# Moving the choice weights, the second score and the row scatter within a step of an attention and expert pipeline

## The reference

```python
x = x + tanh(g_xattn) * cross_attention(layernorm(x), ctx, mask, Wq, Wkv)
x = x + tanh(g_ffn) * experts(layernorm(x), w_router, fc1, fc2, gate_w, up_w, down_w)
```

## Time and profile before

| what | us |
|---|---|
| median of 3 executions | 374.56 |
| lowest and highest | 373.56, 378.98 |
| profiled execution | 375.32 |
| its span in the profile | 373.5 |
| TensorE busy | 312.4 (84%) |
| VectorE busy | 261.0 (70%) |
| ScalarE busy | 170.3 (46%) |
| GpSimd busy | 117.3 (31%) |

### The profile page before, as it was taken

One profiled execution on the slowest core, in us unless ns is written; L12 is line 12 of the kernel. 1 busy time (PEld: TensorE's weight loads), 2 busy tenths in 40 slices (PEclk: granted clock), 3 DMA queues, 4 the chain that ended last, 5 costly groups with the idle time before them and its releaser, 6 DMA issues.

```text
span 373.5 us, 7926 instructions
## 1 busy us (share of the span) xinstructions
PE 312.4 (84%) x2404; PEld 253.7 (68%) x2405; DVE 261.0 (70%) x778; ACT 170.3 (46%) x325; POOL 117.3 (31%) x130
## 2 busy tenths in 40 slices
PE   1827898988998785787979957999898998999994
PEld 1625777776877664553427546888787887888884
DVE  5565587888999698875637996666575665744786
ACT  2413667766675362463355502544343543434231
POOL 4131211216171525234340080564334343332000
PEclk9958999999999896989989996999999999999998
DMA  7728465656569555211020410233233232310783
GB/s 222 207 64 214 113 189 166 182 167 189 175 174 312 164 171 145 94 52 58 34 80 0 119 54 15 85 94 94 85 93 107 72 99 72 96 39 7 237 321 112
DMA packets 34912, 46.44 MB, mean 124 GB/s; under 512 B 5599, under 2 KB 29539, under 8 KB 34370
## 3 DMA queue, kind: packets, MB, share of 16 engines
q1 hardware_dynamic: 28434, 29.17, 27.8%
q10 hardware_dynamic: 2992, 8.32, 6.9%
q0 software_dynamic: 3456, 8.56, 6.7%
HBM read 21.55 MB, written 12.62 MB: 91 GB/s over the span
## 4 chain that ended last, share of the span: by engine, by line
PE 51%; DVE 19%; SPq 11%; DMA 8%; issue 5%; ACT 5%; POOL 1%; DVEq 0%; POOLq 0%; ACTq 0%
PE ps L1462 30%; SPq L345 5%; DMA stacks<-work 4%; SPq L352 4%; PE ps L1350 4%; DVE fc_lo L1049 3%; DVE mx L828 3%; PE ps L1512 3%; DVE fc_lo L1043 2%; PE ps L1428 2%; PE ps L1282 2%; PE ps L1266 2%; PE ps L1184 2%; PE ps L1233 2%; DMA stacks<-mx_t 1%
## 5 line engine op out<-in xcount | busy, mean ns | idle before, releaser
L514 POOL DMA_INDIRECT expert_rows<-v_s,slot_u x39 | 38.3, 982 | 76.8 <-ACT v_s L741 61.1
L828 DVE TENSOR_REDUCE mx<-ps 128x8 f32<-128x1024 f32 x32 | 39.2, 1224 | 16.1 <-PE ps L1233 15.4
L487 POOL TENSOR_TENSOR work<-work 128x512 bf16<-128x512 f32 x16 | 18.5, 1156 | 75.3 <-ACT work L565 75.3
L1462 PE MATMUL ps<-fc_hi,xs_hi 128*128 x78 | 35.3, 452 | 6.2 <-DVE xs_lo L1071 6.2
L1090 DVE TENSOR_TENSOR probs<-ps,probs 128x256 f32<-128x256 f32 x39 | 16.6, 425 | 32.9 <-ACT probs L734 32.8
L596 ACT ACTIVATE probs<-ps 128x1024 f32<-128x1024 f32 x32 | 32.6, 1019 | 13.4 <-PE ps L1266 13.2
L479 POOL DMA_INDIRECT dispatched<-row_s,slot_u x32 | 31.8, 992 | 19.7 <-DVE dest_f L924 10.7
L734 ACT ACTIVATE probs<-ps 128x256 f32<-128x256 f32 x39 | 15.0, 384 | 49.6 <-PE ps L1462 49.6
L1462 PE MATMUL ps<-fc_lo,xs_hi 128*128 x78 | 31.8, 407 | 0.0
L1462 PE MATMUL ps<-fc_hi,xs_lo 128*128 x78 | 31.5, 404 | 0.0
L1233 PE MATMUL ps<-stacks 96*128 96x128 bf16 x256 | 20.6, 225 | 11.3 <-DMA stacks<-work 6.2
(11 more groups left out here) (195 smaller groups left out, 808.4 us busy)
## 6 DMA issues: line engine op xcount, KB each, us to landing
stacks<-work SPq DMA_DIRECT2D x96, 128.0 KB, 3.0
probs<-dispatched SPq DMA_DIRECT2D x39, 129.0 KB, 2.1
fc_s<-in_fc ACTq DMA_DIRECT2D x8, 512.0 KB, 3.5
stacks<-expert_rows SPq DMA_DIRECT2D x4, 1024.0 KB, 6.1
fc_s<-in_fc ACTq DMA_DIRECT2D x8, 256.0 KB, 4.2
ctx_s<-in_ctx_t SPq DMA_DIRECT2D x8, 192.0 KB, 3.2
x_all<-in_x SPq DMA_DIRECT2D x1, 1536.0 KB, 9.1
out<-x_all SPq DMA_DIRECT2D x3, 512.0 KB, 6.7
```

The source lines that it names most:

```text
L487: nc.gpsimd.tensor_tensor(out[:, 2, :], rest, out[:, 1, :], ALU.subtract).then_inc(ready, 1)
L514: nc.gpsimd.indirect_dma_start(ys, bass.IndirectOffsetOnAxis(dst_u[:, r:r + 1], 0), y_out[:, r, :], None, bounds_check=2 * T - 1, oob_is_e ...
L828: nc.vector.reduce_max(mx[:, j, 8 * h:8 * h + 8], ps_s, AX_X).then_inc(max_ok[j][h], 1)
L1462: ins = nc.tensor.matmul(out, a, b, start=first and n == 0, stop=last and n == 2)
```

## The change

On GpSimd the four scatters of dispatch(s - 5) stand ahead of both power2 of a step, where they stood between them. On ScalarE second_score and second_row(·, 1) stand behind norm1 and ahead of exp(·, 0, 1), where they stood behind exp(·, 1, 0). On VectorE weights(s - 5) stands directly behind places(s - 5) and ahead of both norm2, where it stood between rest and maxima(·, 1, 1). No operation is added or removed.

```diff
@@ -489,11 +489,10 @@
             for s in range(STEPS):
-                if live(s - 3):
-                    power2(s - 3, 0)
                 if live(s - 5):
                     dispatch(s - 5)
                 if live(s - 3):
+                    power2(s - 3, 0)
                     power2(s - 3, 1)
@@ -665,6 +664,9 @@
                 if live(s):
                     norm1(s)
+                if live(s - 5):
+                    second_score(s - 5)
+                    second_row(s - 5, 1)
                 if live(s - 3):
                     exp(s - 3, 0, 1)
@@ -672,9 +674,6 @@
                     exp(s - 3, 1, 0)
-                if live(s - 5):
-                    second_score(s - 5)
-                    second_row(s - 5, 1)
@@ -940,6 +939,7 @@
                 if live(s - 5):
                     places(s - 5)
+                    weights(s - 5)
                 if live(s - 4):
                     norm2(s - 4, 0)
                     norm2(s - 4, 1)
@@ -957,8 +957,6 @@
                     rest(s - 1, ps_kq, q_ok[0], q_pc, q_ok[2], q_rest, qr_ok)
-                if live(s - 5):
-                    weights(s - 5)
                 if s == G + 2:
```

## The result

Over six executions of each kernel, taken in the same runs, the changed kernel takes 382.45 us in the median (380.04 to 384.11) and the kernel before 377.06 (373.56 to 378.98). The ratio is 1.0147, with a 95% interval of 1.0084 to 1.021: the change costs 5.5 us, by the interval 3.2 to 7.9 (0.0084 and 0.021 of 377.06). The profiled execution took 382.72 us.

What follows compares the result with a forecast made beforehand. A once-per-step ring through tokens_t, SyncE's transfers, scores(0,0) and VectorE's norm2 was taken as the bound. Delays accumulated over steps 5 to 11 to 4.6 us, on 374.56: 379.2 us, own range 377 to 381.5, 8 in 10 374.0 to 383.5.

Steps and rivals of the forecast that it cites:

- The ring: Once-per-step loop tokens_t, SyncE's issues, landing, scores(0,0), VectorE to norm2; a microsecond added before norm2 lengthens steps 5 to 8.
- Step 5: Weights(0) ahead of norm2 delay the ring by their full 1.13 us.
- The tail: From the table of tiles on nothing changes; the 4.6 us delay is carried to the end.
- Step 6: Weights ahead of norm2 cost the full 1.13 us again, together 2.26.
- Step 7: VectorE's lag and the scatter wait before norm2 vanish, so the total delay is 2.06 us, not 3.39.
- Step 8: Weights ahead of norm2 cost 1.13 us, together 3.19.
- Step 11: Weights(6) make norm2 end at 179.25, so tokens_t starts 0.99 us later; together 4.61.
- The recovery: L924 loses its 0.9 us stall in each of steps 5 to 8; 0.3 to 0.45 returns on pieces(1).
- Parts 2 and 3: ScalarE's second_score and second_row(1) earlier: 0 to 0.9 us; GpSimd's dispatch before power2(0): 0 to 2; both taken 0.
- A: Rival: the ring takes the delay up, giving back 3.6 of the 4.6 us; about 375.5 us; chance 0.20.
- B: Rival: VectorE bounds the staircase, not the ring; -3.2 to -4.8 us, about 370.5 us; chance 0.10.
- C: Rival: longer waits lower TensorE's clock at one more step's head; 4.6 + 3.2, about 382.4 us; chance 0.14.

Runs made afterwards that it cites:

- e5: The kernel before once more, no line changed: 378.45 us against 376.37, ratio 1.0062.
- e10: Changed kernel, weights behind both norm2 in steps 5 to 8, at the old place later: 379.28 us, 1.0056 times the kernel before.
- e6: Changed kernel, weights ahead of norm2 in steps 5 to 8 only, old place later: 381.33 us, 1.0121 times the kernel before.
- e1: Changed kernel with weights back between rest and maxima(1,1), ScalarE and GpSimd still changed: 380.63 us, 1.0027 times the kernel before.
- e2: Changed kernel with dispatch back between the two power2: 385.35 us, 1.0117 times the kernel before.
- e3: Changed kernel with weights behind both norm2, ahead of maxima(0,1), in all steps: 386.64 us, 1.0142 times the kernel before.
- e14: Repeat, word for word, of e3 in another group: 385.77 us, 1.0146 times the kernel before.
- e7: Changed kernel, weights ahead of norm2 in steps 9 to 12 only, old place earlier: 376.33 us, 0.9991 times the kernel before.
- e11: Kernel before with both norm2 ahead of places, nothing else moved: 380.71 us, 0.9991 times the kernel before.
- e12: Kernel before plus twelve small VectorE operations between places and norm2 in steps 5 to 8: 390.59 us, 1.0271 times the kernel before.
- e13: Kernel before plus the same twelve operations as e12, directly behind norm2, in steps 5 to 8: 386.34 us, 1.0155 times the kernel before.
- e4: Kernel before plus six small VectorE operations (1.13 us) between places and norm2 in steps 5 to 8: 384.31 us, 1.0061 times the kernel before.

## Why the prediction was right

The forecast was a cost of 4.6 us, and 5.5 were measured, 3.2 to 7.9 by the interval. The 379.2 us are 3.3 below the measured median; 2.5 of these are the base, which was 374.56 in three executions and 377.06 in six. So 382.45 lies above the forecast's own range of 377 to 381.5 and inside the range of 8 in 10, 374.0 to 383.5. What was right is the direction, the mechanism in its main piece, and the size of the difference; part of the last is luck, as the terms show.

**The ring** held where VectorE has its piece of it. Steps with the weights ahead of norm2 are longer, in two groups (2.95 and 3.03 us over three steps). Step 5 gave 1.13 us of the forecast 1.13. To see where the rest lies, I divide each step at the start of its scores(0,0): the head, from there to tokens_t, holds VectorE's piece, and the rest, from tokens_t to the next scores(0,0), holds SyncE's issues and the landing. The sums over steps 5 to 8, in us:

| profile | weights | heads | rests |
|---|---|---|---|
| before | old place | 16.10 | 53.84 |
| e5 | old place | 15.86 | 54.77 |
| e10 | behind norm2 | 15.25 | 54.07 |
| after | ahead of norm2 | 19.20 | 56.09 |
| e6 | ahead of norm2 | 19.19 | 57.30 |
| e1 | old place | 17.44 | 56.76 |
| e2 | ahead of norm2 | 20.81 | 55.33 |
| e3 | behind norm2 | 16.72 | 59.69 |
| e14 | behind norm2 | 17.46 | 57.62 |

Weights ahead of norm2 lengthen the heads by 3.1 us over the kernel before, 3.3 over e5 and 3.4 in e2 over e1; the forecast for these four steps was 3.19. Behind norm2 the heads are as short as with the old place, in e3 and e14 too. What makes e3 and e14 slow lies in the rests and in the later steps. The rests are 1.3 to 2.3 us longer in the changed kernel than in the two unchanged ones, which no term of mine foresaw, and 1.4 us shorter in e2 than in e1, so single profiles can't say whether the change does this. The tail from tokens_t of step 11 on grew by 0.45 us, so the delay was carried to the end, as said.

**Step 6** gave 0.40 of 1.13 over the kernel before, and 0.98 over e5. From the first k issue to scores(0,0) of the next step the kernel before took 12.58 us (80.07 to 92.65), the changed kernel 11.83 (81.93 to 93.76), and e6 and e10 11.74 and 11.65. SyncE's queue for the six k pieces of step 5, in the changed kernel:

```profile
81.93 3.84 SPq L345 DMA_DIRECT2D stacks<-work  x6
```

In the kernel before these six took 4.49 us, which by the sum is most of the 0.75. But in e6 they took 4.59, and there the stretch was 11.74 all the same, so the longer issues alone don't make a stretch long. Between executions of unchanged work this stretch varies by more than the term: 12.58 and 10.84 us in steps 5 and 6 of the kernel before, 10.73 and 12.21 in e5.

**Step 7 is the term that was too small:** I took a change of -0.2 us, and it was +1.04 over the kernel before, +1.2 over e5. I had credited the change with VectorE's lag at 109.58 and with the 0.40 us that norm2 waited for the scatter. VectorE's and TensorE's timelines of e5, the same kernel, in step 7:

```profile
108.45 1.23 DVE L828 TENSOR_REDUCE mx<-ps 128x8 f32<-128x1024 f32 x1 [0.63 <-PE ps L1233]
...
110.38 0.73 DVE L868 TENSOR_SCALAR row_s<-x_all,mv,rs 128x256 f32<-128x256 f32 x2
111.22 0.63 PE L1304 MATMUL ps<-ident,row_s 128*128 128x128 f32 x4 [0.27 <-issue]
```

VectorE is idle before maxima, norm2 waits for nothing, and tokens_t finds it done. The wait for the scatter is not there, in step 6 neither. The lag is, one step earlier:

```profile
89.65 0.61 PE L1233 MATMUL ps<-stacks 96*128 96x128 bf16 x8
91.30 1.22 DVE L828 TENSOR_REDUCE mx<-ps 128x8 f32<-128x1024 f32 x1
```

VectorE starts maxima 1.65 us after the scores, with no idle time, where 0.65 us is normal. It comes with the shorter of the two stretches above: when the pieces land early, VectorE is the late one. So the credit belongs to steps 6 and 7 together. These took 34.28 us before, 33.54 in e5 and 34.44 in e10, and 35.72 in the changed kernel: +1.3 to +2.2, where my two terms gave +0.93 and two full prices would give 2.26. In the heads of the two steps alone it is +0.8 over the kernel before and +1.0 over e5, so there the credit held. What my sum missed is the rests, +0.7 and +1.1: in each of these two unchanged profiles one landing came early, and in the changed one none did.

In step 7 of the changed kernel a second cause stands beside the weights. TensorE's and VectorE's timelines, and the busy times of the stretch with the granted clock behind them:

```profile
112.45 1.55 PE L1280 MATMUL ps<-probs,v_s 128*32 128x128 f32 x32
115.56 0.74 DVE L867 TENSOR_SCALAR row_s<-x_all,mv,rs 128x256 f32<-128x256 f32 x2
```

```profile
112.90:116.30 3.40, 3.40 (x44) 3.00 (x36) 3.12 (x15) 1.62 (x2) 0.23 (x1) 0.50 0.11 16
```

The values products took 1.55 us, where they take 1.08 in e5: the clock was at its lower level, 1.2 GHz, from 112.9 to 116.3, after TensorE had waited 1.57 us for the landing at 111.82. norm2 ended at 116.30, and tokens_t began at 116.41 without idle time before it. So TensorE's slower products filled the time in which it would have waited for norm2, and cost 0.1 us there at most. e6 has the same (the lower level from 112.7 to 116.1), and before, e5 and e10 have no such stretch in steps 5 to 7.

**Step 8** was forecast at +1.13 and measured at +2.78, +1.0 over e5. VectorE and GpSimd in step 8 of the changed kernel, then TensorE:

```profile
134.97 1.16 POOL L487 TENSOR_TENSOR work<-work 128x512 bf16<-128x512 f32 x1 [3.13 <-ACT work L564]
135.24 0.94 DVE L902 TENSOR_TENSOR slot_p<-oh,slot 128x32 f32<-128x32 f32 x1
...
138.56 0.63 PE L1302 MATMUL ps<-ident,row_s 128*128 128x128 f32 x4 [2.05 <-DVE row_s L867]
```

One operation of the places takes 0.94 us, not 0.19, since the third k piece lies over it, and TensorE waits 2.05. This is not the change's doing: the same operation takes 0.64 us in step 8 of the kernel before and 0.89 in e5. The head of step 8 is 4.30 us in the kernel before, 4.31 in e5 and 5.45 in the changed one and in e6, so it grew by 1.15 and 1.14, as forecast. The other 1.63 us lie between tokens_t of step 7 and scores(0,0): 15.07 us before, 16.70 after, but 16.81 in e5. So they are no more than what two executions of the kernel before differ by.

**Step 11** was forecast at +0.99, and that was the other wrong term. In the changed kernel norm2 was done at 184.51, and TensorE was not:

```profile
180.09 2.71 PE L1348 MATMUL ps<-xt_all,gate_s 128*128 128x512 f32 x4
182.59 2.88 PE L1348 MATMUL ps<-xt_all,up_s 128*128 128x512 f32 x4
...
185.31 0.60 PE L1302 MATMUL ps<-ident,row_s 128*128 128x128 f32 x4
```

These two groups take 1.96 and 1.88 us at the full clock. The slow pair also occurs in e5, the unchanged kernel (3.00 and 2.58 us), so it isn't the change's doing. Seven of the thirteen profiles have it, and in these step 11 lasts 15.60 to 16.51 us; in the six others it lasts 13.96 to 14.30. The move itself costs nothing in steps 9 to 12 that can be measured: e7, 0.9991 (-1.9 to +1.2 us by the interval), against +1.4 forecast for them. So the forecast was too small for steps 6 and 7 and too large behind step 8, and the two errors worked against each other: that is luck, and why the total fits better than its terms.

**The recovery** came, and moved as I said. L924 is back at 0.17 us, and GpSimd's third q piece now lies over pieces. VectorE and GpSimd in the changed kernel, step 5:

```profile
86.74 1.16 POOL L487 TENSOR_TENSOR work<-work 128x512 bf16<-128x512 f32 x1 [8.73 <-ACT work L564]
87.44 0.49 DVE L835 TENSOR_SCALAR mx_pc<-mx 128x16 bf16<-128x16 f32 x1
```

0.49 us, four times, in steps 5 to 8. norm2 waits for no scatter in this profile, as forecast. In the runs this was saving off the path: VectorE is busy 2.8 us less, and the kernel is no faster. The Trainium skill, page "SBUF — State Buffer", section "Who interferes with whom", says that the shared ports are held for a whole instruction. The operations of 0.94, 0.99 and 1.07 us above, on tiles of 4 to 32 columns, agree: each ends within 0.05 us of GpSimd's. Of norm2's 1.57 us in e11 the second operation took 1.24, where it takes 0.41, and ended 0.15 us after GpSimd's.

**Parts 2 and 3** at nothing: e1 (-0.6 to +2.7 us for both) and e2 agree with this.

**The rivals.** A, the ring absorbs it: against it 2.95 and 3.03 us, and the heads. B, VectorE is the bound: against it the same, and e12 against e13; but e13 shows that with some 2.4 us a step more VectorE's own work is longer than a step was. C, the clock: it was 1.00 in steps 5 and 6, so it made no part of what these grew by. It fell in step 7, in both kernels with the weights ahead, hidden there behind norm2, and in e4 and e12 after longer waits. I had it right to weigh it, and had taken 1.68 us idle at 92.65 as evidence that such waits are harmless; after 1.57 us at 111.82 the clock fell. The rival of e3's expectation, that work anywhere ahead of maxima(0,1) costs the same, is not put away: e3 and e14 are as slow as the change by their totals. Against it stand e10, e12 against e13, and the short heads.

## What stays open

Why ScalarE followed TensorE's transpose by 0.7 to 2.6 us in steps 5 and 6 in the first and third group, and by 0.27 in the second and in the first profiles of both kernels. The chain of e14 gives the time to TensorE:

```profile
88.36 1.58 PE ps L1248
```

So it was TensorE's signal that came late, not the landing that this copy also waits for; what held the signal is not shown. How much of e3's and e14's cost lies in the steps from 9 on. What sets the time from tokens_t of step 7 to the scores(0,0) of step 8, 15.07 to 18.70 us. Whether the 1.3 to 2.3 us by which the rests grew belong to the change.

## What to carry to other kernels

Before moving work within an engine's list, ask which other engine waits for what stands behind the new place: here six tiny operations ahead of norm2 lengthened the head of the step by about what they last wherever norm2 feeds the ring of transfers, while 0.9 us a step of real saving on the same engine bought nothing. A stall that shows in one step of one profile may be missing in the next, or stand in another step; before a term takes credit for it (a lag, a wait of 0.4 us, a slow pair of products), look at the neighbouring steps and at a second profile of the same kernel. Where one operation stands between another and a port that two engines share, putting the important one first can bring it under the wait for that port.

## What was not expected of the hardware

An identical kernel read 1.0062 with an interval of 1.0023 to 1.0101, and the kernel before took 376.4 us on the chip of one group and 381 to 382 on those of the two others. The granted clock fell to 0.50 after a wait of 1.57 us, and stayed at 1.00 after one of 2.05 in the next step of the same execution. The two groups of products of the shared expert took 3.9 us together in some executions and 5.6 in others of one and the same kernel.
